# A ten-stage decoder on one core: the layer norm's last step on ScalarE in two stages, one power for three factors, and a maximum over all of x in five parts

## The reference, cut to what matters

```
x = layernorm(x + stage(x))        # (r - mean) / sqrt(var + 1e-5)

# L0_xattn, the channel attention (with the context)
attn = softmax(einsum('bsd,bse->bde', x, ctx) / sqrt(256), axis=1)
y    = einsum('bde,bse->bsd', attn, ctx)

# L2_attn, the cumulative part: three root mean squares of one token
qkv = rms(x) @ w_qkv.T ; q, k, v = split(qkv)
q, k = rms(q), rms(k)              # rms(x) = x * rsqrt(mean(x*x) + eps)
w = exp(k) ; y = sigmoid(q) * cumsum(w*v) / (cumsum(w) + 1e-6)

# L2_ffn: one maximum over the whole of x, one over the weight
xs = max(|x|) ; ws = max(|weight|)
y  = einsum(fp8(x / xs), fp8(weight / ws)) * (xs * ws), to bf16, + bias

# L3_ffn, the last stage: bitlinear(gelu(bitlinear(x, w_fc)), w_proj)
```

## Time and profile before

| | us |
|---|---|
| median of 3 runs (lowest to highest) | 4639.46 (4636.97 to 4642.03) |
| the profiled execution | 4635.98 |
| its span in the trace | 4634.2 |
| PE busy | 4383.5 (95%) |
| DVE busy | 3211.4 (69%) |
| ACT busy | 2081.3 (45%) |
| POOL busy | 1521.3 (33%) |

### The profile page before, as it was taken

The page is one execution under the profiler, slowest core; times in us unless marked ns, Lnnn a source line. Parts: engine busy times, 40 slices in busy tenths (PEclk is TensorE's granted clock), DMA queues, the critical chain, the costliest instruction groups (busy, mean ns, idle before and its releaser), DMA issues.

```text
span 4634.2 us, 87894 instructions
## 1 busy us (share of the span) xinstructions
PE 4383.5 (95%) x32643; PEld 3085.3 (67%) x32643; DVE 3211.4 (69%) x6025; ACT 2081.3 (45%) x4454; POOL 1521.3 (33%) x3105
## 2 busy tenths in 40 slices
PE   8998998799989999997799999999998999999999
PEld 6776998455547777776466666666665666666666
DVE  5668337788888788888555555555555677676698
ACT  4544113355554434333455555555553434444444
POOL 1112004334322233433344444444442323232232
PEclk9999999899999999999899999999999999999999
DMA  1003003444420110000000000000001000000000
GB/s 47 2 22 87 15 1 72 98 90 94 89 46 36 51 33 9 8 8 8 32 1 1 1 1 1 1 1 1 1 1 61 8 11 8 10 8 8 3 16 20
DMA packets 118790, 117.08 MB, mean 25 GB/s; under 512 B 22688, under 2 KB 110560, under 8 KB 113248
## 3 DMA queue, kind: packets, MB, share of 16 engines
q1 hardware_dynamic: 116656, 108.45, 9.2%
q10 hardware_dynamic: 1712, 3.02, 0.2%
HBM read 93.85 MB, written 16.78 MB: 24 GB/s over the span
## 4 chain that ended last, share of the span: by engine, by line
PE 77%; DVE 15%; ACT 3%; issue 2%; DMA 1%; POOL 1%; SPq 0%; ACTq 0%; POOLq 0%; DVEq 0%
PE banks L2512 15%; PE banks L2909 6%; PE banks L1305 5%; PE banks L2762 5%; PE banks L3126 4%; PE banks L791 4%; PE banks L1473 3%; PE banks L1288 3%; PE banks L1987 3%; PE banks L1181 3%; PE banks L2578 2%; PE banks L820 2%; PE banks L2995 2%; PE banks L3095 1%; PE banks L2678 1%
## 5 line engine op out<-in xcount | busy, mean ns | idle before, releaser
L301 POOL TENSOR_TENSOR var_eps<-mean_var,ln_eps 128x1 f32<-128x1 f32 x384 | 77.1, 201 | 1035.2 <-DVE mean_var L297 941.0
L1345 ACT ACTIVATE exps<-banks 128x512 f32<-128x512 f32 x512 | 284.7, 596 | 217.2 <-PE banks L1288 217.1
L1193 DVE TENSOR_REDUCE neg_max<-banks 128x4 f32<-128x1024 f32 x256 | 309.4, 1210 | 86.7 <-PE banks L1181 86.5
L2566 DVE TENSOR_TENSOR q_normed<-banks,factors 128x512 f32<-128x512 f32 x256 | 176.4, 689 | 251.1 <-POOL factors L2556 251.1
L2533 ACT ACTIVATE squares<-banks 128x512 f32<-128x512 f32 x256 | 152.9, 597 | 394.4 <-PE banks L2512 394.4
L1987 PE MATMUL banks<-yT,w_swiglu 128*128 128x128 f32 x2048 | 250.4, 276 | 30.1 <-DVE hidden L2011 28.9
L2556 POOL TENSOR_TENSOR factors<-mean_squares,minus_half 128x4 f32<-128x4 f32 x256 | 258.4, 1010 | 21.4 <-POOL mean_squares L2552 0.2
L1987 PEld LDWEIGHTS banks<-yT,w_swiglu 128*128 128x128 f32 x2048 | 240.6, 192 | 36.5 <-issue 33.2
L2512 PE MATMUL banks<-wq,x_turned 128*128 128x512 f32 x512 | 249.1, 609 | 2.3 <-ACT x_turned L2492 1.9
L2970 POOL TENSOR_SCALAR mean_squares<-square_sums 128x4 f32<-128x4 f32 x160 | 66.0, 413 | 545.9 <-DVE square_sums L2961 545.9
L2909 PE MATMUL banks<-wq,xT 128*128 128x512 f32 x512 | 244.0, 599 | 1.1 <-DVE q_normed L2940 1.1
(11 more groups left out here) (382 smaller groups left out, 10984.1 us busy)
## 6 DMA issues: line engine op xcount, KB each, us to landing
contextT<-in_ctxT SPq DMA_DIRECT2D x96, 128.0 KB, 2.5
parts_context<-parts SPq DMA_DIRECT2D x96, 64.0 KB, 2.5
parts_x<-parts SPq DMA_DIRECT2D x96, 64.0 KB, 2.0
stack<-parts_context SPq DMA_DIRECT2D x32, 192.0 KB
stack<-parts_x SPq DMA_DIRECT2D x32, 192.0 KB
stack<-in_c_fill SPq DMA_DIRECT2D x8, 640.0 KB, 14.9
context<-in_ctx SPq DMA_DIRECT2D x64, 64.0 KB, 2.3
context<-in_ctx SPq DMA_DIRECT2D x32, 128.0 KB, 2.3
```

The source lines that it names most:

```text
L1193: v.tensor_reduce(self.mx[s][:, :, 2 * i:2 * i + 2].rearrange("p h g -> p g h"), self.bM[i % 2].rearrange("p g (h c) -> p g h c", h=DH), A ...
L1345: self.nc.scalar.activation(self.e[n % 8][:], self.bE[self.slot(t, n) % 2].rearrange("p (l c) -> p l c", l=DH), ACT.Exp, scale=self.TOK ** ...
```

## The change

Four things are changed.

1. In the channel attention, the last step of the tail goes from DVE (L307) to ACT (as L325), behind the exponentials in ACT's list. POOL makes the shift as well. DVE's sum waits until the x of two tiles earlier is written, since ACT now reads that buffer.
2. The same in the last stage, where the step is the last in ACT's list.
3. In the cumulative part, rx = (ms + eps)^-0.5 is no longer taken first and multiplied into the others. The other two means are taken with eps * a added, so that one power over three columns gives all three factors: five POOL instructions in place of seven. The first exponential waits for the fourth of them, and the second for the fifth.
4. The maximum over x has five parts: tiles 0 to 7, 8 to 15, 16 to 23, 24 to 29, and 30 to 31. The fourth part is put at tick 284 of the section before, the maximum over the weight at tick 240. `setup_dve` takes only the fifth part and the maximum over the parts. Product, fp8 weight and copy stand behind the first rounding of x.

```
 class ChannelAttention
     def sum_dve(self, dve, t, s):
+        if begun(t - 2):
+            dve.wait_ge(self.x_new.sem, self.x_new.all(t - 2))
         self.tail_sum(dve, t, s, self.bY[s])
+
+    def scale_act(self, act, t, s):
+        self.tail_scale_act(act, t, s, self.r[s][:])
...
-            "act": [(1, self.exp_act)],
-            "dve": [(4, self.sum_dve), (1, self.max_dve), (2, self.normalise_dve), (4, self.tail_scale)],
-            "pool": [(4, self.tail_pool)],
+            "act": [(1, self.exp_act), (4, self.scale_act)],
+            "dve": [(4, self.sum_dve), (1, self.max_dve), (2, self.normalise_dve)],
+            "pool": [(4, self.tail_shift_pool)],
...
 class BitLinearFFN
     def p4_dve(self, dve, t, s):
         dve.wait_ge(self.y_ready.sem, self.y_ready.all(t))
+        if begun(t - 2):
+            dve.wait_ge(self.x_new.sem, self.x_new.all(t - 2))
...
-            "act": [(5, self.down_act), (3, self.norm_act), (2, self.p1_act), (0, self.normx_act), (1, self.p0_act)],
-            "dve": [(6, self.p4_dve), (0, self.in_stats), (4, self.p2_dve), (0, self.p0_dve), (2, self.p1_dve), (6, self.tail_scale)],
-            "pool": [(6, self.tail_pool), (0, self.in_pool), (2, self.p1_pool)],
+            "act": [(5, self.down_act), (3, self.norm_act), (2, self.p1_act), (0, self.normx_act), (1, self.p0_act), (6, self.scale_act)],
+            "dve": [(6, self.p4_dve), (0, self.in_stats), (4, self.p2_dve), (0, self.p0_dve), (2, self.p1_dve)],
+            "pool": [(6, self.tail_shift_pool), (0, self.in_pool), (2, self.p1_pool)],
...
 class CumulativeAttention, scales_pool
-        link(pool.tensor_scalar(self.a[:], self.ss[s][:, 0:1], 1.0 / D, self.EPS, ALU.mult, ALU.add))
-        link(pool.tensor_tensor(rx, self.a[:], self.p.minus_half[:, 0:1], ALU.pow))
-        link(pool.tensor_scalar(self.t1[:], self.ss[s][:, 1:3], rx, rx, ALU.mult, ALU.mult))
-        link(pool.tensor_scalar(self.t2[:], self.t1[:], 1.0 / D, self.EPS, ALU.mult, ALU.add))
-        link(pool.tensor_tensor(self.t3[:], self.t2[:], self.p.minus_half[:, 0:2], ALU.pow))
-        link(pool.tensor_scalar(self.rr[s][:], self.t3[:], rx, None, ALU.mult))
+        link(pool.tensor_scalar(a, self.ss[s][:, 0:1], 1.0 / D, self.EPS, ALU.mult, ALU.add))
+        link(pool.tensor_scalar(self.eps_a[:], a, self.EPS, None, ALU.mult))
+        link(pool.tensor_scalar(self.means[:, 1:3], self.ss[s][:, 1:3], 1.0 / D, self.eps_a[:, 0:1], ALU.mult, ALU.add))
+        link(pool.tensor_tensor(self.factors[s][:], self.means[:], self.minus_half[:], ALU.pow))
         link(pool.tensor_scalar(self.nrq[s][:], self.rr[s][:, 0:1], -1.0, None, ALU.mult))
...
 class Fp8Linear
-        self.prepare = {"dve": [self.part_max(c) for c in range(3)]}
+        self.ends = (0, self.NT // 4, self.NT // 2, 3 * self.NT // 4, self.NT - 2, self.NT)
+        self.prepare = {"dve": [self.part_max(c) for c in range(3)] + [self.weight_max, self.part_max(3)]}
...
-    (together, (Fp8Linear, AlibiAttention), 65.5, 65.5, None, (104, 168, 232)),
+    (together, (Fp8Linear, AlibiAttention), 65.5, 65.5, None, (104, 168, 232, 240, 284)),
```

More of the change, by code:

```diff
@@ L625, in __init__ @@
         self.SCALE = D ** -0.5
+        self.shift = [wk(f"shift{s}", [P, 1]) for s in (0, 1)]
+        self.shift_ready = st("shift_ready")
     def leaves(self):
@@ L1823, in __init__ @@
         self.junk = wk("squares", [P, D])
-        self.a, self.t1, self.t2, self.t3 = wk("a", [P, 1]), wk("t1", [P, 2]), wk("t2", [P, 2]), wk("t3", [P, 2])
-        self.rx = [wk(f"rx{s}", [P, 1]) for s in (0, 1)]
-        self.rr = [wk(f"rq_rk{s}", [P, 2]) for s in (0, 1)]
+        self.means, self.eps_a = wk("mean_squares", [P, 3]), wk("eps_a", [P, 1])
+        self.minus_half = wk("minus_half", [P, 3])
+        self.factors = [wk(f"rx_rq_rk{s}", [P, 3]) for s in (0, 1)]
+        self.rx, self.rr = [f[:, 0:1] for f in self.factors], [f[:, 1:3] for f in self.factors]
         self.nrq = [wk(f"neg_rq{s}", [P, 1]) for s in (0, 1)]
@@ L1841, in __init__ @@
         self.twice_ready = p.once("set_up", 1)
-        self.one, self.one_ready = wk("one", [P, 1]), p.once("zeroed", 1)
-        self.projected = st("projected"); self.squared = st("squared", 3); self.scales = st("scales", 7)
+        self.one, self.one_ready = wk("one", [P, 1]), p.once("zeroed", 2)
+        self.projected = st("projected"); self.squared = st("squared", 3); self.scales = st("scales", 5)
         self.exped = st("exped", 2); self.weighted = st("weighted", 1); self.summed_up = st("scored")
@@ L1918, in exp_act @@
     def exp_act(self, act, t, s):
-        act.wait_ge(self.scales.sem, self.scales.all(t))
+        act.wait_ge(self.scales.sem, self.scales.at(t, 4))
         if begun(t - 1):
@@ L1923, in exp_act @@
         self.nc.scalar.activation(self.ww[:, 1, :], self.bQ[:, D:], ACT.Exp, scale=self.rr[s][:, 1:2]).then_inc(self.exped.sem, 1)
+        act.wait_ge(self.scales.sem, self.scales.all(t))
         self.nc.scalar.activation(self.eq[:], self.bQ[:, 0:D], ACT.Exp, scale=self.nrq[s][:, 0:1]).then_inc(self.exped.sem, 1)
@@ L2292, in setup_dve, with linked, link, weight_max @@
         link(v.tensor_copy(self.wq[:], self.w8[:]))
[L2293 removed]
+    def linked(self, dve, k):
+        count = [k]
+        def link(ins):
+            count[0] += 1
+            ins.then_inc(self.maxes.sem, 1)
+            dve.wait_ge(self.maxes.sem, self.maxes.at(count[0]))
+        return link
     def part_max(self, c):
         def go(dve):
[L2298 to L2303 removed]
+            dve.wait_ge(*self.front.x_new.end(self.ends[c + 1] - 1))
+            x = self.p.x_all[:, self.ends[c]:self.ends[c + 1], :].rearrange("p n d -> p (n d)")
+            self.linked(dve, c if c < 3 else c + 1)(self.nc.vector.tensor_reduce(self.p.part_max[:, c:c + 1], x, AX.X, ALU.max, apply_absolute_value=True))
+        return go
+    def weight_max(self, dve):
+        dve.wait_ge(self.loaded.sem, self.loaded.done)
+        self.linked(dve, 3)(self.nc.vector.tensor_reduce(self.m2[:, 1:2], self.w[:].rearrange("p h n -> p (h n)"), AX.X, ALU.max, apply_absolute_value=True))
     def setup_pe(self, pe):
[L2306 to L2308 removed]
+        pe.wait_ge(self.maxes.sem, self.maxes.at(7))
+        self.nc.tensor.transpose(self.bM[0:2, 0:P], self.m2, self.p.ident[:]).then_inc(self.m_turned.sem, 1)
+        pe.wait_ge(self.maxes.sem, self.maxes.at(9))
         pe.wait_ge(self.ones_set.sem, self.ones_set.done)
@@ L2326, in round_x_dve @@
         self.nc.vector.tensor_scalar(self.x8[s][:], self.bT[:, 0:D], self.inv[:, 0:1], None, ALU.mult, saturate=False).then_inc(self.turns.emptied.sem, 1)
+        if first(t):
+            self.weights_dve(dve)
     def copy_x_act(self, act, t, s):
@@ L3189, in decoder @@
         plan.ps = ctx.enter_context(nc.psum_tensor("banks", [P, 8, 512], F32))
-        plan.part_max = plan.take("always", "part_max", [P, 4], F32)
+        plan.part_max = plan.take("always", "part_max", [P, 8], F32)
         plan.bank = [plan.ps[:, i, :] for i in range(8)]
```

34 lines of the change are left out of this document (12 added, 22 removed).

## The result

| | median, us | runs |
|---|---|---|
| before | 4638.89 (4632.49 to 4644.01) | 8 |
| with the change | 4619.73 (4611.15 to 4625.95) | 8 |

The ratio is 0.9961, with a 95% interval from 0.9952 to 0.9970, which is 14 to 22 us less: faster, with no change well outside the interval. The forecast was 14.0 less than 4639.46, so 4625.5, with 4620.5 to 4632.5 as its range. In a later comparison the same changed kernel came to 0.9958 (0.9945 to 0.9970). So the direction and the order of size are right, and the gain is larger than forecast, 18 to 19 us in place of 14. The forecast gave a gain above 17 a chance of 0.04.

What follows compares the result with a forecast made beforehand. DVE was taken to set the channel attention's step, PE close behind, and to close the last stage's step. Terms -5.6, -6.3, 0 and -2.1 sum to -14.0 us: 4639.46 becomes 4625.5, range 4620.5 to 4632.5.

Steps and rivals of the forecast that it cites:

- Which engine is next in the channel attention: Channel attention: with L307 off DVE, PE becomes the bound at about 2.94 us per step, from 3.21, gaining 0.27.
- How many steps gain: Channel attention: 16 steps from 377 us gain 4.3, the last one 0.3, earlier steps 1.0; sum -5.6 us, range -3 to -7.
- before that, from 340 to 360, ... I take 1.0: Channel attention ahead of the weight transfers: PE lacks 1.58 of 20 us; 1.0 us gained, in from 0 to 1.6.
- The last stage: Last stage: DVE still closes the step, 8.505 to 8.235 us; 0.265 in each of 26 steps, 6.9 us gained.
- The end: Very end, last tile's x: a shift of 0.27 and an ACT step of 0.61 replace DVE's 0.41, costing +0.5 us.
- One power for three factors: Cumulative section, POOL's chain: 0 us, since its result is ready 4.5 us before ACT first uses the factors.
- The maximum in five parts: Section before and start of `Fp8Linear`: weight's maximum costs +0.72, the start gains 2.85; sum -2.1 us, range -0.5 to -3.5.
- Rival 1: Both attention edits pay only in part, as POOL holds up DVE or ACT delays PE: -2 to -4 us, 4635; chance 0.14.
- Rival 2: Only the channel attention or only the last stage gains: 4630 or 4632 us; chance 0.17.
- Rival 3: Cumulative section: PE falls to half its clock in more steps, +1.6 us each; 4665 if 25 fall; chance 0.03.
- the forecast's own case: Whole kernel: all three gains about as computed, 4622 to 4630 us; chance 0.62.
- ACT's higher price: Rule against the change: L325 takes 614 ns on ACT, L307 410 on DVE; 0.2 us lost per tile where ACT sets pace.

Runs made afterwards that it cites:

- a_early: Kernel before, with the channel attention's final scale on ACT only for tiles 0 to 8, the other tiles left on DVE; ratio 0.9986 (0.9977 to 0.9996).
- pool_extra: Changed kernel with three more small POOL instructions behind each shift of the channel attention; step again 2.94 us, no total time given.
- half_max: Changed kernel with the channel attention's maximum reading only half of the columns, about 0.5 us less DVE work per step; step 2.94 us, no total time given.

## Why the forecast was right, and where it was not

* **Which engine is next in the channel attention**: right. 2.94 was forecast and 2.938 measured, with PE full, and two kernels show that PE sets it, and neither DVE nor the scale on ACT. The bound of 2.91 had been read from a single interval behind a stall, where DVE was not in the way; the 0.03 of handover on top was a guess, so the agreement to the hundredth is luck.
* **How many steps gain**: wrong, and the largest miss, -5.6 against -7.7 (-7.4 alone). The failed step is "before that, from 340 to 360, ... I take 1.0", together with "the transfers that follow are issued at a step count and end when they end". Its first half says why the gain stays: an issue at a step count moves with the steps. The first tiles gave 2.8, and `a_early` shows them kept. The upper bound of 1.6 was too low as well: it was drawn from 20 us, 340 to 360, while the ten steps up to the twelfth maximum span 36, and one of them was 0.5 longer before because POOL held up DVE (at 338.66, above). This is 1.8 of the miss of 2.1; the rest is at the stage's end, where 0.7 was gained and 0.3 counted. Only the three steps at the transfers gave nothing or less.
* **The last stage**: right that DVE's slot of L307 was what each step could give back, short in size. The forecast took that slot, 0.27, and a step of 8.235 closed by DVE, with PE at 8.205; measured were 8.19, with PE busy 199.96 of 200. The rest is about 0.05 per step: the addition behind L307 took 0.48 and passed to the next instruction after 0.51, and it takes 0.44 and 0.48 now. Why it is shorter without L307 ahead of it was not tested. DVE shows no wait either, and no experiment takes them apart here, so "DVE still closes the step" stays unproven. What PE shows is that its 0.30 idle per step is gone: 26 times 0.30 is 7.8, and the stretch gave 7.9. Counted on DVE's additions the 27 steps up to the drain give 8.5, of which the first steps of the drain take back 0.6; on PE the drain is the same in both, 26.13 us from the start of the projection L1473 at 4603.37 (L1480 at 4581.72 with the change) to the last addition. The forecast's own terms, 6.9 less 0.5, also make 6.4 and not the 6.3 that it sums.
* **The end**: +0.5 forecast, +0.55 measured, by the durations of the earlier trace rows.
* **One power for three factors**: right, 0. POOL's chain is shorter and nobody waits for it.
* **The maximum in five parts**: right, near enough in each term. Six tiles 1.75 in the gap, two tiles 0.69, the weight's maximum 0.72 forecast and 0.83 measured where the clock held, the start -2.85 forecast and -2.81 measured (-3.1 alone). By the times alone part 4 could be read as -4.8; its interval (-9 to -1) holds the -2.6 of the landmarks.
* **Rival 1** (POOL or ACT takes it back): fell by `pool_extra` and `half_max`. **Rival 2** (one stage only) fell by the kernels with one part each. **Rival 3** (the clock): the mechanism is there, with 1.3 to 1.7 us a fall and up to 3.0 for a long one, but two or three falls in every trace with or without the change, and it is scatter beside 18 us.
* **The chances**: the gain of 18 to 19 lies in the case "a gain larger than 17", which had 0.04, and not in the forecast's own case (4622 to 4630), which had 0.62. The range held, and the engines and waits were named rightly, but parts 1 and 2 were both sized too small, which the chances did not allow for.
* **ACT's higher price**: the step costs ACT 0.61 where DVE paid 0.41, as the Trainium skill's page "ScalarE: Activation LUTs" (Rules for kernel authors) would have it. The rule does not ask which engine is waited for; with 0.52 us still idle on ACT in a step, the dearer instruction was the right one. The Trainium skill's page "Perfetto Trace Analysis" (Optimizing Scalar/DVE Operations) says that where DVE is saturated, work may well go to ScalarE, and the traces agree with it.

## What to carry to other kernels

An instruction taken from a full engine is worth at most the distance to the next engine's own step, and that step can be read where the full engine happens not to be in the way, behind a stall or in a drain. Ask of each stall whether it is tied to the work (an issue at a step, which moves with it) or to a time. The first kind kept what was gained ahead of it; the second would eat it, but no run here has one. Take landmarks from two traces before believing a difference of times: here the scatter at one place, 4.2 us over fourteen traces, was larger than one whole part of the change.

## What was not expected of the hardware

POOL can be held up by DVE, as DVE by POOL above. `in_shift` on POOL (one column) took 0.26 before:

```profile
4503.44 0.26 POOL L1715 TENSOR_SCALAR in_shift<-in_mean_var,in_rstd 128x1 f32<-128x1 f32 x1
```

With the shift ahead of it, it starts at 4485.65, at the same moment as DVE's L1704 (0.75, one SBUF source and one result of 1024 columns), and it takes 0.80: it ends 0.05 behind that one. In 26 of the stage's 32 tiles it takes 0.78 to 0.80, in the rest 0.27. ACT's `x_normed` then waits 0.42 for it, and ends at 4487.08, 0.14 ahead of DVE's next use at 4487.22; a second instruction more on POOL might have cost DVE its full row. This wasn't tried. The Trainium skill ("SBUF — State Buffer", Who interferes with whom) names a pair of ports that VectorE and GpSimd share, with an exclusive lock: whichever instruction starts first holds it to its end, and the other waits. It also says that a DVE instruction with at most one SBUF input, outside the modes with two ports, does not contend. The traces agree in both directions: here L1704 starts first (by 0.01 to 0.03 us) and POOL waits, at 338.60 POOL starts first and DVE's product of two SBUF tensors waits. In `pool_extra` the one of the three instructions that starts while that product runs takes 0.40 in place of 0.26, and nothing on DVE is lengthened.
